# Reordering Pool's queue between a feed-forward layer and the second attention

## The reference

```python
x = x + tanh(g_xattn[0]) * L0_xattn(ctx, layernorm(x), mask, ...)   # 4 heads, keys from context and latents
x = x + tanh(g_ffn[0])   * L0_ffn(layernorm(x), ...)                # 256 -> 1024 -> 1024 -> 256, weights +-1
x = x + tanh(g_xattn[1]) * L1_xattn(layernorm(x), ctx, ...)         # 16 heads of 64, keys from context
x = x + tanh(g_ffn[1])   * L1_ffn(layernorm(x), ...)                # 16 experts, 4 of them chosen, and a shared one
```

```python
q, k, v = h @ Wq, ctx @ Wk, ctx @ Wv            # 16 heads of 64
out = softmax(q @ k.T / sqrt(64)) @ v @ Wo + bo
```

## Time and profile before

| | us |
|---|---|
| median of 3 runs | 1268.04 |
| lowest and highest | 1263.68, 1269.64 |
| the profiled execution | 1265.38 |
| its span | 1263.6 |
| TensorE busy | 1097.2 (87%) |
| VectorE busy | 898.9 (71%) |
| ScalarE busy | 679.8 (54%) |
| Pool busy | 278.6 (22%) |

### The profile page before, as it was taken

How to read it: one execution, slowest core, us unless ns; L and a number is a source line. 1 busy time by engine, 2 the same in 40 slices (tenths; PEclk the granted TensorE clock), 3 DMA queues, 4 the chain that set the end, 5 groups by cost and what they waited for, 6 DMA issues and landing times. The chain is left out here.

```text
span 1263.6 us, 20142 instructions
## 1 busy us (share of the span) xinstructions
PE 1097.2 (87%) x6824; PEld 954.5 (76%) x6824; DVE 898.9 (71%) x1517; ACT 679.8 (54%) x1237; POOL 278.6 (22%) x280
## 2 busy tenths in 40 slices
PE   1869987996699659899898989899997988999998
PEld 1758876885488548788787878788886877888887
DVE  6689838898733648787777778787878866555555
ACT  3467756773211447676675767677777732323222
POOL 5050005003511030402012030402020032344432
PEclk9889989999699979999999999999999988999999
DMA  4000000003101000000100010000000003444332
GB/s 148 1 5 1 1 1 1 2 1 110 27 16 38 1 1 1 2 1 3 36 1 2 1 36 2 1 1 1 27 1 1 1 26 86 112 116 115 103 101 80
DMA packets 18046, 38.20 MB, mean 30 GB/s; under 512 B 3776, under 2 KB 10048, under 8 KB 17440
## 3 DMA queue, kind: packets, MB, share of 16 engines
q1 hardware_dynamic: 17952, 37.01, 10.0%
HBM read 35.76 MB, written 1.25 MB: 29 GB/s over the span
## 5 line engine op out<-in xcount | busy, mean ns | idle before, releaser
L270 PE MATMUL PS<-R 128*128 128x512 f32 (+2 forms) x2728 | 644.1, 381 | 67.6 <-POOL R L424 15.2
L270 PEld LDWEIGHTS PS<-R 128*128 128x128 f32 x2728 | 461.6, 197 | 145.5 <-issue 42.5
L1289 DVE TENSOR_TENSOR R<-PS,R 128x512 fp32r<-128x512 f32 x352 | 225.5, 686 | 62.5 <-ACT R L1022 57.3
L1022 ACT ACTIVATE R<-PS 128x512 fp32r<-128x512 f32 x352 | 190.0, 596 | 146.9 <-PE PS L608 146.8
L608 PE MATMUL PS<-eye,FA 128*128 128x128 f32 x1408 | 188.5, 279 | 40.7 <-ACT FA L998 31.2
L608 PEld LDWEIGHTS PS<-eye,FA 128*128 128x128 f32 x1408 | 155.0, 141 | 74.7 <-issue 26.3
L619 PEld LDWEIGHTS PS<-R 128*128 128x128 f32 x1408 | 186.0, 189 | 26.4 <-issue 11.7
L619 PE MATMUL PS<-R 128*128 128x256 f32 x1408 | 193.4, 283 | 8.6 <-DVE FB L1297 8.3
L998 ACT ACTIVATE FA<-PS,nmax 128x1024 f32<-128x1024 f32 (+1 forms) x160 | 193.0, 1206 | 3.4 <-DVE nmax L1278 3.4
L1278 DVE TENSOR_REDUCE nmax<-PS 128x1 f32<-128x1024 f32 x128 | 155.6, 1216 | 16.6 <-PE PS L270 11.5
L424 POOL TENSOR_SCALAR R<-R 64x512 fp32r<-64x512 f32 x40 | 26.1, 654 | 432.9 <-ACT R L1139 371.0
(11 more groups left out here) (159 smaller groups left out, 1038.2 us busy)
## 6 DMA issues: line engine op xcount, KB each, us to landing
FB<-comb SPq DMA_DIRECT2D x48, 256.0 KB, 3.8
wst<-we_in SPq DMA_DIRECT2D x26, 384.0 KB, 4.0
wst<-w_in SPq DMA_DIRECT2D x4, 1024.0 KB, 5.0
wst<-w_in SPq DMA_DIRECT2D x3, 512.0 KB, 6.3
x<-x_in SPq DMA_DIRECT2D x2, 512.0 KB, 5.7
FB<-ctxT_in SPq DMA_DIRECT2D x2, 512.0 KB, 4.6
FB<-k_in SPq DMA_DIRECT2D x8, 128.0 KB, 2.4
FB<-ctxT_in SPq DMA_DIRECT2D x4, 256.0 KB, 3.9
```

Source lines behind the costliest of these rows:

```text
L270: last = mm(out, a, b, start=(n == 0), stop=(n == len(passes) - 1), skip_group_check=skip)
L1022: a_(L.pt[0][:, (u // 2) % 2, 4 * g_:4 * g_ + 4, (u % 2) * P:(u % 2) * P + P], L.turn(u, g_).rearrange("p (t n) -> p t n", t=4), ACT.Copy) ...
L1289: inc(v.tensor_tensor(lo, turned, hi.bitcast(F32), ALU.subtract), "p_lo")
```

## The change

The loop that added both biases ahead of everything else becomes a function that is called for each batch apart. Pool now zeroes the spare query rows first, then adds batch 0's bias, makes the low part of the keys (`pair1_low`), copies the queries, and adds batch 1's bias last. Each bias add is followed by a wait of Pool for its own count.

```diff
-        for b in range(NB):
+        def add_bias(b):
             pool.wait_ge(s["ln_xn"], 2 * NB + NB + b + 1)
             pool.wait_ge(s["bo_gated"], 2)
             for t in range(TT):
                 last = g.tensor_tensor(x[:, b * TT + t, :], x[:, b * TT + t, :], bo[:, :], ALU.add)
             last.then_inc(s["bo_added"], 1)
+            pool.wait_ge(s["bo_added"], NB + b + 1)
 
         pool.wait_ge(s["f2_done"], 2 * MT)
-        pool.wait_ge(s["bo_added"], 2 * NB)
         zero_spare_queries(L1, 4)
+        add_bias(0)
+        pair1_low(2, 5)
         copy_queries(L1, 2, 14)
-        pair1_low(2, 5)
+        add_bias(1)
         with pool.Fori(1, NG1) as i:
```

## The result

| | before | after |
|---|---|---|
| median of 8 runs | 1268.44 us | 1258.51 us |
| lowest, highest | 1263.68, 1272.48 | 1249.89, 1264.07 |
| the profiled execution, its span | 1265.38, 1263.6 us | 1258.23, 1256.4 us |

The ratio of after to before is 0.9924, with a 95% interval of 0.9898 to 0.995: faster by 0.8%, that is by 6.3 to 12.9 us of 1268.44. Timing alone can't tell a gain of 7 us from one of 12; the traces must.

What follows compares the result with a forecast made beforehand. TensorE, busy 1097.2 of 1263.6 us (87%), was taken as the bound, so its waits are what can be lost. -10.43 + 0.6 = -9.8 us, from a mean of 1266.7, gave 1257 us, range 1252 to 1262.

Steps and rivals of the forecast that it cites:

- 1.: Zeroing ahead of batch 0's bias: its 1.95 us are hidden, but memsets delay VectorE's last feed-forward subtraction, +0.6 us.
- 2.: Key subtractions ahead of the copies: they run in Pool's idle time with 6 us to spare, cost 0.
- 3.: Query copies before the second attention start 0.19 us after the queries; first score matmul comes 10.43 us earlier.
- 4.: First maximum of the second attention: VectorE's normalization ends 0.19 us ahead and is late next.
- 5.: Batch 1's bias last on Pool: ends before VectorE needs it for its loop, 3.0 us of slack, cost 0.
- 6.: First scores still run at 1.2 GHz after a 4.8 us stop; the clock's effect is at most 0.19 us.
- Rival A: Around the moved copies, Pool and VectorE hold each other more: gain 6.9 us, 1260 us; chance 0.08.
- Rival B: Between the attention heads, stops tip TensorE's clock, some 1.7 us per fall: slower or no gain; chance 0.08.
- Rival C: Behind the stop, something with its own pace takes the gain back: gain 0 to 6 us; chance 0.07.
- one sign of being wrong: In the new profile: the stretch from the first scores to the end changes by more than 2 us.

Runs made afterwards that it cites:

- e3: Changed kernel with the zeroing done by an instruction that reads its tile and multiplies by 0; VectorE's last feed-forward subtraction took 1.40 us in place of 0.69.
- e2: Changed kernel with memsets behind batch 0's bias and key subtractions behind the copies; first turn 35.95 us after the feed-forward's last subtraction, against 32.75.
- e10: Changed kernel with the key subtractions behind batch 1's bias; 1251.95 us in one profiled execution, normalization to first turn 5.56 us against 5.59.
- e5: Changed kernel with the first two query copies started after the first query job; first maximum 28.52 us after the feed-forward's last subtraction, against 28.74.
- e4: Changed kernel with eight 128x1024 memsets between the copies and batch 1's bias; first turn 35.79 us after the feed-forward's last subtraction, against 32.75.
- e9: Changed kernel with 14 matmuls on a zero tile in TensorE's stop; the eight score matmuls took 2.06 us in place of 3.75.
- a3: Changed kernel, unedited, timed a second time (6 runs) and traced; ratio to before 0.9916, medians 1268.67 and 1256.42 us.
- e1: Kernel before with only the memsets moved ahead of both bias adds; 1264.98 us in one profiled execution, TensorE's stop 13.22 us against 15.25.
- e8: Changed kernel with early query copies, first maximum ahead of batch 1's normalization and exponential table loaded early; ratio to before 0.9913.

## Why the prediction was right

The forecast, 1257 (1252 to 1262) and 9.8 us less, met 1258.51 and a difference of medians of 9.9 us. The traces confirm the mechanism of the gain (steps 2 to 4). That the two numbers agree to 0.1 us is luck: the interval of the timing is 6.3 to 12.9 us, the second timing has medians 12.2 apart, and one term of the sum was wrong by 0.6. By its steps:

1. The zeroing hides in Pool's idle time: right. What it does to VectorE's last subtraction: predicted +0.6, measured 0 (0.69 us in all traces with memsets there). The mechanism was sized by a row of an instruction that reads; e3 gave the reading kind its 0.7 and so shows that the place was right and the kind of instruction wrong. The forecast's sentence on the Trainium skill's rule (SBUF — State Buffer, "SBUF: two separate sides") came nearer with 0.1: only the cast was touched, 0.45 us in place of 0.43, and Pool's two memsets took 2.12 us in place of 1.95.
2. The subtractions hide: right for the place where they went, 5.37 us. But I priced them at 0 against a kernel in which they stood behind the copies, and didn't ask what they would have done there. Before the change the normalization was long over when they ran (452.89 against 444.53); with the second bias out of the way they would have met it. e2 shows 3.2 us at the first turn. Moving them away from there, ahead of the copies here or behind the bias in e10, is worth 3.2 of the 10.4 us; the forecast had no term for it.
3. The copies were to start 0.19 us behind the queries and TensorE 10.43 us sooner: measured 0.18 (437.32 to 437.50) and 10.41.
4. The next limit is VectorE's normalization, 0.19 us ahead: 0.20 measured, and e5 shows it binding.
5. 3.0 us of slack for the second bias: it ends at 445.67, VectorE is ready at 448.67, so 3.0. What happens beyond it is only half shown (e4).
6. The clock falls in the new stop too and costs at most 0.19 us: the scores took 3.75 us in both, and e9 gives 0.17.

Rival A (VectorE and Pool holding each other) cost nothing to speak of in the changed kernel, but it is real: e2, e3 and e4 each show VectorE held when an instruction gets the wrong neighbour. Rival B, that the clock might tip in the stretches between the heads, was right in that the clock moves the result by microseconds. It was mostly wrong in the place: the largest part lay ahead of T and between the first experts and the router, and only 0.8 us, in a3, in the first turns between the heads. Its price of 1.7 us for the fall around 424 was too high: runs without that fall (e1, e9, e10) reach the normalization 0.96 to 0.98 us sooner. Three traces of the changed kernel are too few to say that the clock treats both kernels alike; two of them are as good as before in the expert stretch. Rival C found nothing: the way from the twelfth turn to the experts is the same to 0.8 us in all three traces.

The forecast named one sign of being wrong that did show: a stretch from the first scores to the end changed by more than 2 us. It was 810.5 us before and 815.5 in the first trace of after. In the other two it is 811.4 and 810.7, so the sign was the clock between experts and router, which the forecast had not reckoned with as a source of 4 us.

The sum of -10.41 and 0 is 0.6 us more than forecast. It can't be seen in medians of kernels whose runs scatter by 9 to 14 us.

## What to carry to other kernels

Take an engine that does not bound the time but whose queue mixes urgent and late work. Ask of each piece which data it needs and when these were there. The gap between that time and its start is what a new order can gain, and it came out here to 0.02 us at the first matmul. Then look at the second arrival before counting it, and at the neighbours: Pool instructions moved next to VectorE instructions of the wrong kind cost 0.7 to 3.2 us at the first turn here. And when one kernel's runs scatter more than the effect, measure from a fixed event ahead of the edit to one behind it, in more than one trace.

## What the runs showed of the hardware that I had not expected

- Which pairs hold each other. A VectorE subtraction with both inputs in SBUF: free beside a memset (0.69 us), held beside Pool's reading multiply (1.40). VectorE's one-input instructions in SBUF (normalization, 1.38 us for four): held beside memsets (3.68) and beside Pool's subtractions (4.75), and a 128x4 one took 1.00 in place of 0.17. Those with an input in PSUM were not held in any row shown, nor were the batch-norm statistics, which read SBUF, beside Pool's copies (1.41 for four).
- The time of one kernel goes with the granted clock of the run: 1249.89 us at a mean of 0.973 and 1264.07 at 0.957 for the changed kernel, the ends of its 8 runs.
- The same stop need not have the same effect on the clock. Behind a stop of 2.2 to 2.3 us the mean granted clock of the stretch from T + 6 to T + 12 us was 0.72 before and 1.00 in e1, and the way to the normalization 27.14 and 26.18 us. Behind the second turn's wait of 2.2 us the turn took 1.09 us before and 1.96 in e1.
- A sooner start can be given back. From the first to the third turn it took 7.25 us after the change (32.75 to 40.00) and 8.77 in e8 (30.57 to 39.34): 0.70 of it is the wait for the second exponential and 0.82 lies behind the second turn, which ran at 1.2 GHz.
